# Shared expert blocks split in two runs, RWKV and attention blocks with freed buffers, and new order tables

## The reference

```python
x = x + _L0_attn_ref(_layernorm(x), ...)          # Mamba-2 (SSD) with a short convolution, 4 heads of 128
x = x + _L0_xattn_ref(_layernorm(x), ctx_512, ...)  # latent cross-attention, 16 heads
x = x + _L0_ffn_ref(_layernorm(x), ...)           # 7 routed experts, 2 per token, and one shared expert
x = x + _L1_attn_ref(_layernorm(x), ...)          # RWKV: token shift, k, v, r, WKV recurrence, output
x = x + _L1_xattn_ref(_layernorm(x), ctx_512, ctx_512)  # grouped attention, 32 query heads of 8
x = x + _L1_ffn_ref(_layernorm(x), ...)           # 64 gates, top 8, 8 groups of a masked gated MLP
```

## Time and profile before

| | |
|---|---|
| median of 3 runs | 1988.67 us (1986.06 to 1990.58) |
| the profiled execution | 1992.37 us |
| its span, first to last instruction | 1990.6 us |
| mean granted TensorE clock | 0.988 |
| TensorE matmuls busy | 95% (15,824 instructions) |
| TensorE weight loads busy | 75% |
| VectorE busy | 69% |
| ScalarE busy | 50% |
| POOL busy | 31% |

### The profile page before, as it was taken

One profiled execution on the slowest core, in us unless ns is written; L12 is line 12 of the kernel. 1 busy time (PEld: TensorE's weight loads), 2 busy tenths in 40 slices (PEclk: granted clock), 3 DMA queues, 4 the chain that ended last, 5 costly groups with the idle time before them and its releaser, 6 DMA issues.

```text
span 1990.6 us, 41874 instructions
## 1 busy us (share of the span) xinstructions
PE 1883.3 (95%) x15824; PEld 1501.7 (75%) x15824; DVE 1379.3 (69%) x3622; ACT 1003.0 (50%) x1984; POOL 622.2 (31%) x991
## 2 busy tenths in 40 slices
PE   6999999999999989999978899999999999999999
PEld 5888888888888779998866566667766666776666
DVE  3677888778868645444678777787767778777732
ACT  1455556555555544444534554555555455555552
POOL 1434343444434640100333333233333323323200
PEclk9999999999999999999998999999999999999999
DMA  6320000001421363323211000000000000000200
...
DMA packets 79638, 107.60 MB, mean 54 GB/s; under 512 B 15440, under 2 KB 62544, under 8 KB 79056
## 3 DMA queue, kind: packets, MB, share of 16 engines
...
...
## 4 chain that ended last, share of the span: by engine, by line
PE 77%; DVE 10%; ACT 5%; issue 3%; POOL 3%; DMA 2%; SPq 0%; DVEq 0%; ACTq 0%; POOLq 0%
PE ps L2038 16%; PE ps L385 7%; PE ps L1406 6%; PE ps L766 6%; PE ps L823 5%; PE ps L1431 3%; PE ps L2030 3%; PE ps L444 3%; PE ps L1528 2%; PE ps L1739 2%; PE ps L783 2%; PE ps L1766 2%; PE ps L1538 1%; DVE arena L1573 1%; PE ps L796 1%
## 5 line engine op out<-in xcount | busy, mean ns | idle before, releaser
L2038 PE MATMUL ps<-EARLY,arena 128*128 128x352 f32 x512 | 167.3, 473 | 0.0
L2038 PE MATMUL ps<-EARLY,BIG 128*128 128x352 f32 x512 | 166.8, 472 | 0.0
L1406 PE MATMUL ps<-arena 128*128 128x128 f32 x1136 | 140.3, 279 | 10.5 <-DVE arena L1466 3.5
L1406 PEld LDWEIGHTS ps<-arena 128*128 128x128 f32 x1136 | 135.6, 193 | 16.5 <-issue 7.6
L385 PE MATMUL ps<-arena,EARLY 128*128 128x256 f32 x640 | 147.8, 382 | 0.2 <-DVE small L480 0.2
L1657 POOL DMA_INDIRECT arena<-results_by_slot,posi x64 | 63.3, 990 | 266.9 <-DVE X L1610 140.8
L2038 PEld LDWEIGHTS ps<-EARLY,arena 128*128 128x128 f32 x512 | 94.4, 192 | 65.3 <-issue 22.6
L2038 PEld LDWEIGHTS ps<-EARLY,BIG 128*128 128x128 f32 x512 | 94.5, 192 | 64.7 <-issue 21.8
L1486 ACT ACTIVATE arena<-ps,BIG 128x128 f32<-128x128 f32 x304 | 92.8, 368 | 88.6 <-PE ps L1406 86.7
L385 PEld LDWEIGHTS ps<-arena,EARLY 128*128 128x128 f32 x640 | 119.0, 190 | 15.8 <-DVE small L480 0.6
L1264 POOL DMA_INDIRECT rows_by_slot<-staged,posi x64 | 63.4, 990 | 128.4 <-DMA staged<-rows_by_token 103.7
...
## 6 DMA issues: line engine op xcount, KB each, us to landing
arena<-rows_by_slot SPq DMA_DIRECT2D x38, 256.0 KB, 2.8
results_by_slot<-arena SPq DMA_DIRECT2D x38, 256.0 KB, 2.1
...
rows_by_token<-BIG SPq DMA_DIRECT2D x16, 256.0 KB, 3.2
columns_by_block<-BIG SPq DMA_DIRECT2D x16, 256.0 KB, 3.4
staged<-rows_by_token SPq DMA_DIRECT2D x16, 256.0 KB, 3.0
arena<-columns_by_block SPq DMA_DIRECT2D x16, 256.0 KB, 3.0
```

The source lines that it names most:

```text
L1406: m = e.matmul(ps[:, f * P:f * P + P], L.W[q][:, w:w + P], src[:, q, c * P:c * P + P], start=c == 0, stop=c == 1, skip_group_check=True)
L2038: m = e.matmul(ps[:, 0:352], L.hT[:, c, ts], WG[:, c, g * 352:g * 352 + 352], start=False, stop=c == 1, skip_group_check=True)
```

## The change

Shared blocks 0 to 7 keep their two buffer sets; blocks 8 to 15 become a run of their own, `late`, with one set (columns 5120 and on of arena 2, and the front of two groups of constants that s1, s2 and the tables have used up), whose first load waits for both tables and for shared blocks 6 and 7. In every shared block the products are written over hT. s4 and s5 of block 0 no longer wait for the last shared blocks. s4 and s5 count their steps in two semaphores each; s4 gathers into the flats GV and E2 once the block before has made `num`, and its other buffers are guarded by the steps that read them last; s5 has two KA, and OT and O in places of their own, with BV loaded apart. The second set of s6 moves from column 5632 of BIG to 3520. All numbers of START and TURNS are new. Left out of the diff are those numbers but for two entries, and the five lists of pieces, which get the `late` run behind `shared`.

```diff
--- before.py
+++ after.py
@@ -17,6 +17,7 @@
 NB = 4
 NBLK = NT // TB
 CUT = 12
+LATE = 8
 NPAIR = (27, 11)
 NJ = 2 * sum(NPAIR)
 NEG = -1.0e38
@@ -45,88 +46,92 @@
 
 
 
...
 TURNS = {
...
-    "s5": {"pe": (7.41, -48.18, 11.91, 16.57, 20.99, 39.59, 44.53, -7.39, 48.57, 59.26, -53.37, 63.85),
-          "dve": (-0.73, 1.8, 13.47, 12.64, 21.08, -323.48, 53.77, -66.01),
-          "act": (8.55, -196.86, 20.37, 42.72, -366.59, -231.43, -120.91, 48.14, 44.02, 56.75),
-          "pool": (-61.22, -120.49, -4, -73.65),
-          "sp": (-65.68,)},
+    "s5": {"pe": (8.32, -503.84, 13.5, 20.87, 24.44, 42.77, -1.91, -59.31, 47.24, 52.18, -124.56, 56.14),
+          "dve": (-0.28, 2.81, 13.32, -207.37, 25.07, -547.83, 56.87, -211.85),
+          "act": (13.17, -208.82, 22.23, 48.48, -461.35, -300.76, -416.41, 49.55, -7.88, 53.77),
+          "pool": (-28.19, -651.45, 0.84, -90.85),
+          "sp": (-51.72, -11.94)},
...
+    "late": {"pe": (11.93, 22.56, 46.09),
+          "dve": (26.33, 44.92),
+          "act": (18.74, 25.76),
+          "sp": (-42.13,)},
...
@@ -1267,24 +1272,40 @@
             L = Lane(AR[i])
-            L.hT, L.u, L.zz = (L.cut(512).rearrange("p (k n) -> p k n", k=2) for _ in range(3))
+            L.hT = L.cut(512).rearrange("p (k n) -> p k n", k=2)
+            L.u = [L.cut(256) for _ in range(2)]
             sh.append(L)
+        L = Lane(AR[2], 5120)
+        L.hT = L.cut(512).rearrange("p (k n) -> p k n", k=2)
+        L.u = [groups["c1"][:, 0:256], groups["c2"][:, 0:256]]
+        sh.append(L)
+
+        def sh_lane(n):
+
+            return sh[n % 2 if n < LATE else 2]
+
         shv = steps("shv", 2, "zr x")
...
         def sp_shared(e, n):
-            L = sh[n % 2]
-            if n >= 2:
+            L = sh_lane(n)
+            if n < 2:
+                e.wait_ge(*s1v.at(NBLK - 2 + n, "x1"))
+            elif n < LATE:
                 e.wait_ge(*shv.at(n - 2, "x"))
+            elif n == LATE:
+                for p in range(2):
+                    e.wait_ge(*tbv[p].at(0, "pB"))
+                    e.wait_ge(*shv.at(LATE - 2 + p, "x"))
             else:
-                e.wait_ge(*s1v.at(NBLK - 2 + n, "x1"))
+                e.wait_ge(*shv.at(n - 1, "x"))
             e.wait_ge(*l_cols.at(n))
...
         def pe_shared(e, n):
-            L, k = sh[n % 2], lambda g: ("sh", n, g)
+            L, k = sh_lane(n), lambda g: ("sh", n, g)
             ps = bank.take("sh", k("u"), sha, n, "u")
@@ -1299,7 +1320,7 @@
                 for c in range(2):
-                    m = e.matmul(ps[:, f * 256:f * 256 + 256], UG[:, c, f * P:f * P + P], L.u[:, c, :], start=c == 0,
+                    m = e.matmul(ps[:, f * 256:f * 256 + 256], UG[:, c, f * P:f * P + P], L.u[c], start=c == 0,
                                  stop=c == 1, skip_group_check=True)
@@ -1308,30 +1329,32 @@
                 for c in range(2):
-                    m = e.matmul(ps[:, i * 256:i * 256 + 256], L.zz[:, c, i * P:i * P + P], UD[:, c, :], start=c == 0,
+                    m = e.matmul(ps[:, i * 256:i * 256 + 256], L.hT[:, c, i * P:i * P + P], UD[:, c, :], start=c == 0,
                                  stop=c == 1, skip_group_check=True)
...
         def dve_shared(e, n):
-            L, k, t0 = sh[n % 2], lambda g: ("sh", n, g), n * TB
+            L, k, t0 = sh_lane(n), lambda g: ("sh", n, g), n * TB
             e.wait_ge(*sha.at(n, "zz"))
-            e.tensor_tensor(L.zz[:, :, :], L.zz[:, :, :], L.u[:, :, :], ALU.mult).then_inc(*shv.sig(n, "zr"))
+            for c in range(2):
+                m = e.tensor_tensor(L.hT[:, c, :], L.hT[:, c, :], L.u[c], ALU.mult)
+            m.then_inc(*shv.sig(n, "zr"))
             yield
...
         def act_shared(e, n):
-            L, k = sh[n % 2], lambda g: ("sh", n, g)
+            L, k = sh_lane(n), lambda g: ("sh", n, g)
             e.wait_ge(*bank.full(k("u")))
             for f in range(2):
-                m = e.activation(L.u[:, f, :], bank.of(k("u"))[:, f * 256:f * 256 + 256], ACT.Identity,
+                m = e.activation(L.u[f], bank.of(k("u"))[:, f * 256:f * 256 + 256], ACT.Identity,
                                  bias=moe_b[:, 0, 7, f:f + 1])
...
             for f in range(2):
-                m = e.activation(L.zz[:, f, :], bank.of(k("g"))[:, f * 256:f * 256 + 256], ACT.Silu,
+                m = e.activation(L.hT[:, f, :], bank.of(k("g"))[:, f * 256:f * 256 + 256], ACT.Silu,
                                  bias=moe_b[:, 1, 7, f:f + 1])
@@ -1500,10 +1523,10 @@
         L4.D = L4.h.rearrange("p k (b s) -> p k b s", b=NB)
-        L4.ya, L4.yb = (L4.mx[j].rearrange("p k b s -> p (k b s)") for j in (1, 2))
-        s4v = steps("s4v", 1, "y00 y01 y10 y11 stat aggr var nm mix0 mix1 mix2 MX e1 c d den num d1 o1 d2 d3 rec oo x")
-        s4a = steps("s4a", 1, "h hT K V ee1 R ee2 e2 e1")
-        s4g = steps("s4g", 1, "zz rs mr t0 t1 t2 E2 C gv o2 o3")
+        L4.ya, L4.yb = (L4.flat[name][:, 0:512] for name in ("GV", "E2"))
+        s4v = steps("s4v", 2, "y00 y01 y10 y11 stat aggr var nm mix0 mix1 mix2 MX e1 c d den num d1 o1 d2 d3 rec oo x")
+        s4a = steps("s4a", 2, "h hT K V ee1 R ee2 e2 e1")
+        s4g = steps("s4g", 2, "rs mr zz t0 t1 t2 E2 C gv o2 o3")
         l_comb = Loads(sem("l_comb"), 4)
@@ -1614,6 +1637,9 @@
             quad = lambda g: bank.of(k(g))[:, :].rearrange("p (k b s) -> p k b s", k=2, b=NB)
+            if n:
+                e.wait_ge(*s4v.at(n - 1, "d2"))
+                e.wait_ge(*s4g.at(n - 1, "o2"))
             act_h(e, s4a, s4g, L, n)
@@ -1644,25 +1670,29 @@
                 exs[0].stored(e)
-                e.wait_ge(*shv.at(NBLK - 2, "x"))
+                e.wait_ge(*shv.at(LATE - 2, "x"))
                 e.wait_ge(*tbv[1].at(0, "pB"))
...
             else:
-                e.wait_ge(*s4v.at(n - 1, "x"))
+                e.wait_ge(*s4v.at(n - 1, "num"))
             if n == CUT:
...
                     e.indirect_dma_start(y[:, i * 256:i * 256 + 256], None, ys_d[n // CUT], idx).then_inc(*l_comb.sig())
+            yield
+            pool_rs(e, s4v, s4g, L, n)
+            if n:
+                e.wait_ge(*s4v.at(n - 1, "d2"))
             for w, val in ((L.H, 0.0), (L.K, NEG), (L.E1, 0.0), (L.E2, 0.0), (L.GV, 0.0)):
...
             m.then_inc(*sig("zz"))
-            yield
-            pool_rs(e, s4v, s4g, L, n)
             for j in range(3):
...
                 e.wait_ge(*s4a.at(n, "hT"))
+                if n:
+                    e.wait_ge(*(bank.full(("s4", n - 1, "o")) if j == 1 else s4v.at(n - 1, ("d3", None, "oo")[j])))
                 if n == 0 and j == 0:
@@ -1692,25 +1722,29 @@
         L5.PT = L5.cut(2048).rearrange("p (q b g n) -> p q b g n", q=4, b=2, g=4)
-        L5.KA = L5.cut(512).rearrange("p (b l) -> p b l", b=NB)
+        L5.KA = [L5.cut(512).rearrange("p (b l) -> p b l", b=NB) for _ in range(2)]
         L5.BV = L5.cut(512).rearrange("p (b q c) -> p b q c", b=NB, q=4)
-        L5.OT = [L5.hq[:, i, :, :, :].rearrange("p g k c -> p (g k c)") for i in range(TB)]
-        L5.O = [L5.QT[:, i, 0:2, :].rearrange("p g n -> p (g n)") for i in range(TB)]
+        L5.OT = [EARLY[:, 6336 + 512 * i:6848 + 512 * i] for i in range(TB)]
+        L5.O = [EARLY[:, 7360:7616], sb("attended", 256)[:, :]]
         L5.sums = [L5.sm(32).rearrange("p (g k) -> p g k", g=4) for _ in range(TB)]
         quads = range(4)
-        s5v = steps("s5v", 1, "stat aggr var hn m00 m01 m02 m03 m10 m11 m12 m13 rc0 O0 rc1 O1")
-        s5a = steps("s5a", 1, "qa0 qa1 qb0 e00 e01 e02 e03 qb1 ot0 e10 e11 e12 e13 ot1")
-        s5g = steps("s5g", 1, "zq rs xa0 xa1")
-        l_c5 = Loads(sem("l_c5"), 2)
+        s5v = steps("s5v", 2, "stat aggr var hn m00 m01 m02 m03 m10 m11 m12 m13 rc0 O0 rc1 O1")
+        s5a = steps("s5a", 2, "qa0 qa1 qb0 e00 e01 e02 e03 qb1 ot0 e10 e11 e12 e13 ot1")
+        s5g = steps("s5g", 2, "zq rs xa0 xa1")
+        l_ka = [Loads(sem(f"l_ka{i}")) for i in range(2)]
+        l_bv = Loads(sem("l_bv"))
 
         def sp_s5(e, n):
+            if n >= 2:
+                e.wait_ge(*bank.full(("s5", n - 2, "w13")))
+            else:
+                e.wait_ge(*shv.at(LATE - 1, "x"))
+                e.wait_ge(*exs[0].l_out[1].at((NPAIR[0] - 2) // 4))
+            e.dma_start(L5.KA[n % 2][:, :, :], t["ka"][n, :, :, :]).then_inc(*l_ka[n % 2].sig())
+            yield
             if n:
                 e.wait_ge(*bank.full(("s5", n - 1, "pv1")))
-            else:
-                e.wait_ge(*shv.at(NBLK - 1, "x"))
-                e.wait_ge(*exs[0].l_out[1].at((NPAIR[0] - 2) // 4))
-            e.dma_start(L5.KA[:, :, :], t["ka"][n, :, :, :]).then_inc(*l_c5.sig())
-            e.dma_start(L5.BV[:, :, :, :], t["bv"][n, :, :, :, :]).then_inc(*l_c5.sig())
+            e.dma_start(L5.BV[:, :, :, :], t["bv"][n, :, :, :, :]).then_inc(*l_bv.sig())
             yield
@@ -1727,7 +1761,7 @@
                 if i == 0:
-                    e.wait_ge(*l_c5.at(n))
+                    e.wait_ge(*l_ka[n % 2].at(n // 2))
```

(25 more changed lines are left out.)

153 lines of the change are left out of this document (78 added, 75 removed), and 8 rows, old and new, of the table START.

## The result

The changed kernel takes **1954.97 us** (median of 4 runs, 1953.26 to 1958.93) beside 1989.62 for the kernel before (4 runs): a ratio of **0.983**, 95% interval 0.9805 to 0.9854.

A forecast was written before the change was run, and what follows sets the result against it. TensorE was taken as the bound, with only 107 us of waits to win. Terms -7 (steady run), -5, -2.5, -2.5 and -1 sum to -18, so 1988.7 becomes 1970.7 us; range 1956 to 1992.

The forecast's parts named there:

- The exponential: Steady run: second half of attend can't start before the exponentials end; a new wait of 1.3 us a block.
- The SP rival: Late shared blocks' loads hold SP's queue, so expert pairs wait for rows; slower, 2003 us; chance 0.14.
- Hand-over: 550 to 732 us: eight shared blocks instead of six begin before the first expert pair; -2.5 us, bounds +4 and -6.
- second expert part: 932 to 1065 us: sum ahead of RWKV's chain, last shared block inside the stretch; -5 us, bounds 0 and -12.
- Filling and run-off: Filling, 1065 to 1110 us: scores, M1 and attend go before a 6.0 us wait; -2.5 us, bounds 0 and -6.
- only the 107 us in which it waits can be won: Whole kernel: TensorE is busy 1883.3 of 1990.6 us and no matmul is removed, so only its waits can shrink.
- Removed: up to 2.34: Steady run: the new order takes away the seven named TensorE waits, up to 2.34 us a block.
- net 0.54: Steady run: 2.34 us removed less 1.8 of new waits a block, times 13 blocks: -7 us, bounds -20 and +2.
- period under 56.2: Steady run: a block period below this, against 56.8 forecast, would mean a smaller exponential wait than forecast.
- More is won: Larger gains in steady run (-13 us), second part (10), hand-over (4) and filling's waits and clock; 35 us in all, 1954; chance 0.20.
- Start ... -1 us: Start of the kernel: first weights are issued ahead of X; -1 us, bounds +2 and -3.
- Partly permits: RWKV and attention buffers, gather included: they free nothing on TensorE's path by themselves and only permit another order.

The follow-up runs named there:

- e2b: Changed kernel, its buffers kept, with the old order for most of the last pipeline; 1999.49 us, 0.9823 of the kernel before.
- e3: Kernel before, with X's first load moved behind the six weight loads; 2027.47 us, 0.9993 of the kernel before on its chip.
- e5: Changed kernel, with transposes at11 and at12 back behind RWKV's projections; 1959.74 us, 0.9869 of the kernel before.
- e6b: Changed kernel, with the gather for RWKV's next block late on GpSimd, its new wait kept; 2015.16 us, 1.0116 of the kernel before.

## Why the prediction was wrong

**Right.** All seven waits of the earlier trace rows are gone, and e2b brings them back with the order; none of them hung on a buffer, on kind A (for B see e2b). The exponential is what is late next. L1466's 3.5 us of the earlier trace rows are gone, and the wait of the output projection is in their place, 2.1 us. The SP rival's sign, expert pairs that wait for rows, is nearly absent: 0.6 us between 730 and 920, where it was 2.8 before.

**Right in sum, wrong in place, and partly luck.** Hand-over, experts and second part gave 6.6 of the forecast 7.5, but 2.4 to 10.7 over three traces. The second expert part was to give 5 and gave nothing: TensorE misses 21.1 us there instead of 19.8. The hand-over and the experts gave it instead (14.3 to 9.3 and 7.0 to 2.9). The named waits of the earlier trace rows fell as planned, and others took their place; after, 920 to 1050 (L1429, L1454, L1561 are L1406, L1431, L1538 of before):

```profile
PE ps L1429 <- ACT arena L1509: 5.2, 4, 2.0
PE ps L1429 <- issue: 3.7, 5, 1.5
PE ps L1454 <- DVE arena L1483: 2.5, 3, 1.3
PE ps L1561 <- DVE arena L1630: 2.1, 1, 2.1
```

The first two were 2.3 and 0.9 us before (932 to 1110). The shared block that I laid into this stretch is also longer than I made it: L1293's 13.2 us are seven blocks with one of three groups each, so 5.7 us a block and not 4.6. Filling and run-off gave 2.3 of 2.5, but 1.5 of it is the round behind the thirteen, which takes 52.8 us before with a fall of the clock and 51.3 in e3 without one.

**Wrong: "only the 107 us in which it waits can be won".** In the sum it nearly holds: TensorE's idle time fell by 36.1 of the 39.2 us. But busy time too held something to win, half clock and likely waiting inside groups, and the next two misses come from it.

**Wrong: the removed waits of the steady run, "Removed: up to 2.34".** The new waits were sized well: I put them at 1.8 a block, and they measure 0.76 at M1, 0.8 inside attend and, by all groups of scores (38.3 us before, 43.2 after, 16 blocks), 0.3 inside scores, 1.9 in all. The term "net 0.54" should have been 1.29, because about 0.8 more was removed than the list of waits names: TensorE's busy time in an undisturbed block went from 55.0 to 55.3 us although attend and scores grew by 1.1. e5 shows 0.2 of this, at the transposes. Over four undisturbed rounds (1508.6 to 1737.9 before, 1482.4 to 1706.6 after) the matmuls of u (L2038, L2080) are busy 82.8 and 81.1 us, 0.4 a round less, and the transposes at (L2049, L2091) 12.7 and 11.8, 0.2 less; that this was waiting inside the groups is likely but not shown. I had taken the list of named waits for all the waiting. Thirteen blocks make this 10 us. The sign I had named for a period under 56.2, an exponential wait smaller than I made it, reads it wrongly: the period is 56.04, and M1's wait and attend's stretch make 1.6, no less than my 1.3.

**Wrong: the clock, which the forecast put at nothing.** Mean clock times span gives what it costs: (1 - 0.988) x 1990.6 = 23.9 us before, (1 - 0.992) x 1951.4 = 15.6 after, 8 us less, 6.3 of them in the thirteen rounds. (This is one trace of before; its other executions on A have clocks of 0.985 to 0.991, those of the changed kernel 0.991 to 0.996.) The rival "More is won" had 4 us from the clock and looked for them in the filling, with the rule of the Trainium skill (TensorE: Matmul & The Clock Gate, "Why this matters for your kernels") that idle gaps of several us bring the half clock. The filling's 6.0 us wait is gone, and the clock there is no better (0.79 over 40 us, 0.81 over 45 before). The rule doesn't explain what happened on this trace; the gain came from a stretch whose longest wait was 1.1 us. So the rival's 1954 is met by luck: its 10 us in the second part and 8 in the filling did not come.

**Wrong: "Start ... -1 us".** It gave 7.3 (5.4 to 10.5 over three traces). I had priced the load of X by nothing but its place in a list. DMA moves 171 GB/s in the first 50 us, 232 in the first 10, and X's first load is 512 KB: by my estimate 2.3 to 3 us of exactly what the first matmul waits for. The profile had these numbers. It measured 4.6 to 5.5, and what makes it more than the bytes was not looked into.

In all, the 39.2 us between the traces are 21 more than the forecast 18. The thirteen rounds make 16 of them (10 by waits, 6 by the clock) and the start 6; the rest gave 1 less than forecast.

**A limit.** "Partly permits" was too weak for the gather: without its early place the new order loses 63 us (e6b). I called that "up to 5 us a block" without its cover for the output projection; it was 5.6 in most rounds, which meets the number by luck: 2.2 of it are waits, for the normalisation of the last stage, and most of the rest is the clock.
